# Which engine evicts the fourth bank of attention scores in four steps of a batch

## What is computed

```python
def kernel_func(q, k):
    scores = jnp.einsum('bhqd,bhkd->bhqk', q, k) / jnp.sqrt(HD)
    w = jax.nn.relu(scores)
    return w / (jnp.sum(w, axis=-1, keepdims=True) + KERN_EPS)

x = x + 0.5 * _L0_ffn_ref(_layernorm(x), ...)      # "pre": silu(h @ w1 + b1) @ w2 + b2, residual
x = x + _L0_attn_ref(_layernorm(x), ...)           # 16 heads of 8, B = 8 batches, S = 512
x = x + 0.5 * _L0_ffn_ref(_layernorm(x), ...)      # "post"
```

## Time and profile before

| | us |
|---|---|
| median of 3 runs | 370.36 |
| lowest, highest | 370.11, 371.77 |
| profiled execution | 370.82 |
| its span, first to last instruction | 368.9 |

### The profile page before, as it was taken

One profiled execution on the slowest core, in us unless ns is written; L12 is line 12 of the kernel. 1 busy time (PEld: TensorE's weight loads), 2 busy tenths in 40 slices (PEclk: granted clock), 3 DMA queues, 4 the chain that ended last, 5 costly groups with the idle time before them and its releaser, 6 DMA issues.

```text
span 368.9 us, 11764 instructions
## 1 busy us (share of the span) xinstructions
PE 359.7 (98%) x4524; PEld 185.4 (50%) x4524; DVE 287.8 (78%) x689; ACT 231.2 (63%) x425; POOL 218.2 (59%) x447
## 2 busy tenths in 40 slices
PE   8999998999999999999999999999999999999996
PEld 8854433444465445653464444644456534532475
DVE  5876677997878977799777978789787787678874
ACT  3377466657846577566866578465775668688523
POOL 7695065547963589337892479635893376315551
PEclk9999999999999999999999999999999999999999
DMA  6016006400452006400172003610063001700001
GB/s 208 8 32 172 3 0 142 117 3 2 101 130 60 3 4 149 135 4 1 38 186 69 4 0 85 147 60 0 9 161 94 4 0 39 192 30 2 2 4 60
DMA packets 14103, 22.66 MB, mean 61 GB/s; under 512 B 2528, under 2 KB 3808, under 8 KB 14048
## 3 DMA queue, kind: packets, MB, share of 16 engines
q1 hardware_dynamic: 11456, 17.83, 19.9%
q10 hardware_dynamic: 2592, 4.07, 3.3%
HBM read 3.54 MB, written 2.10 MB: 15 GB/s over the span
## 4 chain that ended last, share of the span: by engine, by line
PE 86%; DVE 4%; DMA 3%; ACT 2%; issue 2%; POOL 2%; SPq 0%; DVEq 0%; POOLq 0%; ACTq 0%
PE o_bank L682 31%; PE scores L659 16%; PE post_bank L603 9%; PE pre_bank L603 9%; PE pre_bank L608 5%; PE pre_bank L609 3%; DMA s_rows<-in_L_ffn_fc_scales_dram 2%; PE post_bank L608 2%; PE pre_bank L631 2%; PE pre_bank L596 2%; PE post_bank L609 2%; PE post_bank L631 2%; PE post_bank L596 1%; PE pre_bank L698 1%; DMA q_op<-q_parts 1%
## 5 line engine op out<-in xcount | busy, mean ns | idle before, releaser
L1280 DVE TENSOR_SCALAR probs<-scores 128x512 f32<-128x512 f32 x242 | 155.6, 682 | 44.6 <-PE scores L659 40.1
L981 ACT ACTIVATE probs<-scores 128x512 f32<-128x512 f32 x262 | 141.6, 596 | 64.8 <-PE scores L659 64.7
L682 PE MATMUL o_bank<-probs,v_op 128*32 128x512 f32 x1024 | 135.9, 602 | 0.2
L659 PE MATMUL scores<-q_op,k_op 32*128 32x512 f32 x504 | 76.0, 494 | 1.4 <-ACT probs L981 0.6
L659 PEld LDWEIGHTS scores<-q_op,k_op 32*128 32x128 f32 x504 | 32.0, 181 | 81.5 <-issue 54.1
L870 ACT ACTIVATE pre_y<-pre_bank,b_sum,col_consts 128x512 f32<-128x512 f32 x28 | 21.8, 780 | 23.6 <-PE pre_bank L631 23.6
L682 PEld LDWEIGHTS o_bank<-probs,v_op 128*32 128x32 f32 x1024 | 22.0, 108 | 28.4 <-issue 24.4
L603 PE MATMUL pre_bank<-w,pre_y 128*32 128x128 f32 x960 | 30.8, 274 | 0.0
L603 PEld LDWEIGHTS pre_bank<-w,pre_y 128*32 128x32 f32 x960 | 25.7, 110 | 8.1 <-issue 7.6
L603 PE MATMUL post_bank<-w,post_y 128*32 128x128 f32 x960 | 29.4, 273 | 0.0
L603 PEld LDWEIGHTS post_bank<-w,post_y 128*32 128x32 f32 x960 | 25.9, 110 | 5.7 <-issue 5.4
(11 more groups left out here) (219 smaller groups left out, 557.2 us busy)
## 6 DMA issues: line engine op xcount, KB each, us to landing
k_op<-k_parts SPq DMA_DIRECT2D x62, 128.0 KB, 2.6
q_op<-q_parts SPq DMA_DIRECT2D x62, 128.0 KB, 2.7
out_dram<-o_rows ACTq DMA_DIRECT2D x7, 256.0 KB, 2.0
pre_x<-in_x_dram ACTq DMA_DIRECT2D x6, 256.0 KB, 2.8
w_int<-in_L_ffn_fc_q_dram SPq DMA_DIRECT2D x2, 256.0 KB, 3.8
rows<-in_lines_dram ACTq DMA_DIRECT2D x1, 256.0 KB, 6.7
s_rows<-in_L_ffn_fc_scales_dram SPq DMA_DIRECT2D x1, 256.0 KB, 7.2
wqk<-in_w_qk_dram SPq DMA_DIRECT2D x1, 256.0 KB, 7.3
```

Of the source, the lines that this page charges most:

```text
L659: mm(score_bank(b, s, i, j), k_op[rows, g, P * kt:P * (kt + 1)], q_op[rows, g, :], start=True, stop=True).then_inc(scores_done[i], 1)
L682: last = mm(o_bank[pair][VW * j:VW * (j + 1), :], v_op[:, kt, heads_of(g).start + 2 * j, :], probs[:, s % 2, j, :], start=(odd == 0 and kt ...
L981: activation(probs[:, s % 2, 2 * i + j, :], score_bank(b, s, i, j), ACT.Relu).then_inc(probs_done[i][j], 1)
L1280: v.tensor_scalar(probs[:, s % 2, 2 * i + j, :], score_bank(b, s, i, j), 0.0, None, ALU.max).then_inc(probs_done[i][j], 1)
```

## The change

In batches 1 to 6 ACT evicts three of the four banks in steps 3, 6, 8 and 10, and DVE one, and in batch 0 in steps 6, 8, 9 and 10; all other steps have two each. Batch 7 keeps its nine steps of three. The bank that moves is (1,1), and `by_dve`, which takes what `by_act` leaves, follows. That is 28 evictions in all. Where ACT takes the bank over from DVE it first waits for DVE's count on that bank (`act.wait_ge(probs_done[i][j], ...)`, L980). No order of tasks is changed, no task is moved, and the banks stay as they are.

```diff
-THREE_BY_ACT = (0, 1, 2, 3, 4, 8, 9, 10, 14)
+
+THREE_BY_ACT = {0: (6, 8, 9, 10), B - 1: (0, 1, 2, 3, 4, 8, 9, 10, 14)}
+THREE_ELSE = (3, 6, 8, 10)
...
 def by_act(b, s):
 
-    return [(0, 0), (0, 1), (1, 1)] if b == B - 1 and s in THREE_BY_ACT else [(0, 0), (0, 1)]
+    return [(0, 0), (0, 1), (1, 1)] if s in THREE_BY_ACT.get(b, THREE_ELSE) else [(0, 0), (0, 1)]
```

## The result

| | us |
|---|---|
| before, median of 7 runs | 370.93 |
| after, median of 7 runs | 372.80 (372.41 to 373.38) |
| ratio after/before, 95% interval | 1.0061, 1.005 to 1.0073 |
| profiled execution after, its span | 372.74, 370.9 |

The account below looks back on a forecast made before the run. Only time on PE's queue was taken to move the end, with evictions bounding some steps without filler. Six middle batches at +0.43 and batch 0 at -0.08 gave +2.5 us, a median of 372.9 us, range 371.8 to 373.9.

Parts of the forecast that it names:

- The sum: Whole kernel: +0.43 us in each of six middle batches, +2.58, and -0.08 in batch 0, together +2.5 us.
- The signs named for it: New profile, middle batch: steps 3 to 11 20.8 us, 6.47 from step 8's first score, score rows 1.28, 0.50, 0.75.
- The busy times: 28 evictions change engine: DVE falls by 19 us of busy time, ACT gains 17, and the time gets no better.
- The loop of 1.98 and 2.23: Bank (1,1)'s next score, steps without filler: 1.98 us after the first score with DVE's pair, 2.23 with three on ACT.
- Steps 8, 9 and 10: Batches 1 to 6: step 9's last score moves 0.24 us, step 11's last score comes 0.49 later, and that stays.
- Step 3: Batches 1 to 6: DVE's 0.19 us wait goes, but fc2.0 waits for ACT's last silu, so the gain is 0.06.
- (a): Rival: the silu doesn't hold fc2.0, so step 3 gives 0.18 us and not 0.06; 372.1 us, chance 0.12.
- Step 6: Costs and brings nothing: ACT's third eviction ends a microsecond ahead of step 7's scores, covered by 64 fc2 matmuls.
- Batch 0: Steps 6, 8, 9, 10: of 0.45 us won in step 10, the next step takes all but 0.08; -0.08.
- (b): Rival, scores on bank (1,1) in steps 9 and 11: only DVE's lateness costs; 369.3 to 370.0 or 364.7 us; chance 0.08.
- (c): Rival: the granted clock falls as PE waits up to 0.8 us in step 11; adds 17 us, 390; chance 0.02.

Follow-up runs that it names:

- step 10 alone: Three banks by ACT only in step 10 of batches 1 to 6, against the kernel before: 372.22 us against 370.49, ratio 1.0043.
- half an eviction less: Changed kernel with ACT's third eviction covering 256 of 512 columns in batches 0 to 6: 368.90 us against 370.35 of before, ratio 0.9954.
- without the statistics: Kernel before with x1's statistics measured on one tile of four in batches 1 to 7: 370.20 us against 370.49, ratio 0.9987.
- step 8 alone: Three banks by ACT only in step 8 of batches 1 to 6, against the kernel before: 372.21 us against 370.49, ratio 1.0031.
- step 7: Three banks by ACT only in step 7 of batches 1 to 6, against the kernel before: 371.44 us against 370.35, ratio 1.0031.

## Why the prediction was right

**The sum** held in size and in place. A middle batch was to take 0.43 more and takes 0.42; six were 2.58 and are 2.53. The signs named for it came out one by one: 20.83 us for the nine steps, 6.45 from step 8's first score to step 11's last, rows of 1.28, 0.51 and 0.74 for the scores of steps 11, 10 and 9, ACT as the releaser, and steps 12 to 2 unchanged. The forecast of 372.9 stands beside 372.8. Part of that closeness is luck: it was made from a median of 370.36, the seven runs of before that the result goes by have 370.93, and the measured difference is 1.9 to 2.3 us where 2.5 was forecast. What lies between isn't the mechanism. The two traces' spans differ by 1.96 us: the six batches add 2.53, the stretch ahead of the first score 0.34 (it starts at anything from 20.44 to 22.09 in the fourteen kernels), batch 0 takes off 0.8 (below), and batch 7 with the end 0.2.

**The busy times** were sized too high: DVE was to fall by 19 us and ACT to gain 17, and it is 15.5 and 13.1. The working took an eviction's own length, 0.68 and 0.60, where evictions that follow each other overlap and cost one pitch, 0.61 and 0.49, as its own section on three banks had it: 28 of these are 17 and 14. The time doesn't rest on it.

**The loop of 1.98 and 2.23.** This was the step of the working that decided, and the one without a row of its own. Step 11's last score is 2.23 after step 10's first in the changed kernel, 2.22 with step 10 alone and 2.02 with half an eviction less. With DVE's pair it is 1.98 whether DVE was late before (the kernel before) or not (1.97 without the statistics, 1.98 with step 8 alone). The halved eviction, which keeps the semaphores and the order, shows the length of ACT's turn to be the cause.

**Steps 8, 9 and 10.** Step 9's last score moved by 0.24, step 10's lateness vanished, and it was worth nothing, as worked out: 0.23 and 0.26 for the two steps by themselves against 0.24 and 0.25.

**Step 3.** The silu holds fc2.0 as said, and the gain is 0.06. (a) is out, as the halved eviction confirms: with an earlier silu the gain is 0.17.

**Step 6** costs nothing, and step 7 shows that the cover is the reason. The sentence that step 6 without its cover would cost what step 10 does was put on step 7, which has none: 0.22.

**Batch 0.** Steps 8 to 11 are 0.07 shorter, and 0.08 was the forecast. Missed was step 7, another 0.2 (below). The trace of after has batch 0 shorter by 0.5 us more in step 15, where the q copy's DMA is waited for; by such waits the kernels of the experiments differ in this step by anything from -0.6 to +0.1, with two banks or three, and it is no part of the change as far as these runs show.

**Rivals.** (b) is out at both of its places: ACT's third eviction ends at 2.17 and not by 1.93, and DVE's lateness taken away alone wins nothing in a middle batch, so there it wasn't even a price (in batch 0 it was one of 0.4). The occupancy rule of the Trainium skill (Perfetto Trace Analysis, Identifying the Most-Contended Engine), by which the prediction named DVE, points the wrong way in this kernel: DVE was relieved of 15.5 us and 2 us were lost. (For TensorE the section puts the share of peak FLOP/s beside the weight loads; the prediction went by the weight loads alone.) (c) didn't happen: the granted clock is 1.000 over the changed kernel's span, with waits of 0.79 inside step 11's scores.

## What to carry to other kernels

Where two engines share the emptying of one step's banks, as here, the step's loop is as long as the longer turn, counted from the first result and not from the engines' busy shares; a bank moves to the less busy engine without cost where the producer has other work that outlasts the new turn. A wait seen in a trace is worth winning only if what comes behind it isn't bound by something that began before the wait: take it away by itself first, even by leaving out work that the result needs. A filler that looks free to move may be the cover of another chain, and the bank it writes has its own last reader.

## What had not been expected of the hardware

ACT's first eviction of step 7 in batch 0 starts 0.3 us late after a long idle. The kernel before, and the changed one, ACT's rows:

```profile
41.34 1.08 ACT L981 ACTIVATE probs<-scores 128x512 f32<-128x512 f32 x2 [3.27 <-PE scores L659]
```

```profile
41.36 1.08 ACT L983 ACTIVATE probs<-scores 128x512 f32<-128x512 f32 x2 [2.46 <-PE scores L661]
```

The step's first score is at 40.45 in the first and at 40.78 in the second, so ACT starts 0.89 after it where it had idled for 3.27 us, and 0.59, the usual, after 2.46. The same holds in all fourteen kernels: 0.89 to 0.91 after 3.26 to 3.28 us of idle in the eleven that have two banks on ACT in step 6 of batch 0, 0.59 after 2.46 to 2.69 in the three that have three. A third eviction in step 6 thus goes with a step 7 that is 0.2 us shorter.

The length of the idle time alone doesn't do it. Near the end of the kernel before, PE's transposes and the copy of them that ACT makes after 3.94 us of idle:

```profile
356.91 0.38 PE L737 MATMUL pre_bank<-ident,post_h 128*128 128x128 f32 x2
...
357.33 0.38 ACT L921 ACTIVATE post_t_hi<-pre_bank 128x256 fp32r<-128x256 f32 x1 [3.94 <-PE pre_bank L737]
```

It starts 0.04 after the end of PE's row, and in step 11 of batch 3 a copy of transposes starts 0.03 after such an end (174.65 + 0.66) at 175.34, after 0.65 us of idle. Something else does fall in the stretch of the late start: the traces hold a transfer of 8 KB on queue q14, which carries instructions. In the eleven kernels with the late start it begins 0.64 to 0.68 us behind that start (at 42.00 before), in the other three 2.2 to 2.4 us ahead of step 7's first score (at 38.54 after), beside step 6's evictions. Whether the late start and this transfer have to do with each other wasn't tried; ACT isn't late wherever such a transfer falls (one begins at 124.52 before, and the evictions ahead of it start 0.59 after their step's first score), and the cause stays open.
